# A twelve-block transformer on one core: the narrow heads' weighted values and the wide output projection, each as one TensorE step per block

## The reference

```python
h = layer_norm(x) * (1 + scale) + shift            # scale, shift from cond
q, k, v = h @ Wq, ctx_or_h @ Wk, ctx_or_h @ Wv      # split into 16 heads
a = softmax(q @ k.T / sqrt(dh))                     # 16 maps of 128 x 128
x = x + concat(a @ v) @ Wo + bo                     # gated in layer 3
...
x = x + act(h @ W1 + b1) @ W2 + b2                  # gelu, or silu(h@W1)*(h@W3)
```

## Time and profile before

| | |
|---|---|
| median of three runs | 1695.45 us |
| the profiled execution's own time | 1690.91 us |
| its span | 1688.9 us |
| TensorE matmul busy | 1518.5 us (90%), 15228 records |
| VectorE busy | 1403.1 us (83%), 3745 instructions |
| ScalarE busy | 1095.0 us (65%) |
| GpSimd busy | 911.7 us (54%) |
| mean granted TensorE clock | 0.97 of full speed |

### The profile page before, as it was taken

One profiled execution on the slowest core, in us unless ns is written; L12 is line 12 of the kernel. 1 busy time (PEld: TensorE's weight loads), 2 busy tenths in 40 slices (PEclk: granted clock), 3 DMA queues, 4 the chain that ended last, 5 costly groups with the idle time before them and its releaser, 6 DMA issues.

```text
span 1688.9 us, 40850 instructions
## 1 busy us (share of the span) xinstructions
PE 1518.5 (90%) x15228; PEld 1196.7 (71%) x15228; DVE 1403.1 (83%) x3745; ACT 1095.0 (65%) x4765; POOL 911.7 (54%) x1028
## 2 busy tenths in 40 slices
PE   6988999999889989999988989999989999989875
PEld 5876777677667777777766767776767778767653
DVE  5878788988997778898898868998898888888864
ACT  1766778657565777756576667766666686775632
POOL 3746454555765546455566646545575664554432
PEclk9999999999999999999999999999999999999975
DMA  9100000000000000000000000000000000000000
GB/s 328 37 1 2 2 2 2 7 4 4 7 8 2 2 1 2 2 7 7 6 3 7 2 2 2 2 7 1 7 7 7 2 2 2 2 2 3 3 1 3
DMA packets 14437, 20.91 MB, mean 12 GB/s; under 512 B 4064, under 2 KB 10784, under 8 KB 14240
## 3 DMA queue, kind: packets, MB, share of 16 engines
q1 hardware_dynamic: 14240, 18.31, 3.3%
HBM read 17.25 MB, written 1.05 MB: 11 GB/s over the span
## 4 chain that ended last, share of the span: by engine, by line
PE 47%; DVE 38%; POOL 8%; ACT 5%; issue 2%; DMA 0%; SPq 0%; POOLq 0%; ACTq 0%; DVEq 0%
DVE negmax L1007 9%; PE ps L665 9%; PE ps L691 6%; PE ps L552 6%; PE ps L704 5%; POOL E L859 5%; DVE E L1108 4%; ACT E L752 4%; DVE xn L967 3%; PE ps L678 3%; DVE E L1060 3%; PE ps L629 3%; PE ps L643 2%; PE ps L576 2%; PE ps L567 2%; PE ps L655 2%
## 5 line engine op out<-in xcount | busy, mean ns | idle before, releaser
L752 ACT ACTIVATE E<-ps,negmax 128x128 f32<-128x128 f32 x2048 | 719.3, 410 | 261.9 <-DVE negmax L1007 249.4
L859 POOL TENSOR_TENSOR E<-E,rinv 128x512 f32<-128x512 f32 x512 | 525.2, 1042 | 375.3 <-DVE rinv L1016 373.2
L752 ACT ACTIVATION_READ_ACCUMULATOR E<-ps,negmax 128x1 f32 x2048 | 509.7, 250 | 0.0
L1007 DVE TENSOR_REDUCE negmax<-ps 128x4 f32<-128x512 f32 x512 | 330.1, 680 | 59.3 <-PE ps L629 33.8
L665 PE MATMUL ps<-consts,E 128*128 128x128 f32 x2048 | 316.8, 285 | 39.7 <-POOL E L859 24.1
L1108 DVE COPY E<-ps 128x512 f32<-128x512 f32 x448 | 299.8, 678 | 54.6 <-PE ps L665 52.4
L665 PEld LDWEIGHTS ps<-consts,E 128*128 128x128 f32 x2048 | 233.0, 144 | 116.0 <-POOL E L859 67.6
L852 POOL TENSOR_TENSOR E<-E,prod 128x512 f32<-128x512 f32 x128 | 162.3, 1274 | 73.9 <-DVE prod L1063 72.2
L807 POOL TENSOR_TENSOR rstd<-ve,consts 128x1 f32<-128x1 f32 (+1 forms) x192 | 107.9, 563 | 83.5 <-DVE ve L960 74.0
L691 PE MATMUL ps<-E,VV 128*64 128x128 f32 x2048 | 139.4, 282 | 2.2 <-DVE E L1108 2.1
L761 ACT ACTIVATE VV<-ps 128x512 f32<-128x512 f32 x128 | 77.3, 671 | 89.8 <-PE ps L567 89.5
(11 more groups left out here) (130 smaller groups left out, 2757.1 us busy)
## 6 DMA issues: line engine op xcount, KB each, us to landing
w_f<-res_f SPq DMA_DIRECT2D x6, 256.0 KB, 11.5
qT<-in_x SPq DMA_DIRECT2D x16, 64.0 KB, 1.8
w_wq<-res_wq SPq DMA_DIRECT2D x2, 512.0 KB, 7.8
w_wk<-res_wk SPq DMA_DIRECT2D x2, 512.0 KB, 8.4
w_wv<-res_wv SPq DMA_DIRECT2D x2, 512.0 KB, 9.1
w_wo<-res_wo SPq DMA_DIRECT2D x2, 512.0 KB, 9.8
w_cq<-res_cq SPq DMA_DIRECT2D x2, 512.0 KB, 10.8
w_co<-res_co SPq DMA_DIRECT2D x2, 512.0 KB, 13.7
```

The source lines that it names most:

```text
L752: last = nc.scalar.activation(E[p][:, h, :], bank(u, j * N, (j + 1) * N), ACT.Exp, bias=negmax[p][:, h:h + 1], accum_out=sums[p][:, h:h + 1])
L859: tt(e, e, rinv[p][:, T4 * g:T4 * g + T4].unsqueeze(2).broadcast_to([N, T4, N]), ALU.mult).then_inc(done[POOL], 1)
L1007: nc.vector.tensor_reduce(negmax[p][:, T4 * g:T4 * g + T4], bank(u).rearrange("p (h m) -> p h m", h=T4), AX, ALU.max, negate=True).then_in ...
```

## The change

The four steps `MX0` to `MX3` of a narrow block become one step `MX`, which comes after all four turned groups and the values and does the same sixteen matmuls in the same order. The steps `PJ0` and `PJ1` of a wide block become one step `PJ`, which comes after both copies and does the same eight matmuls. Their costs in the plan are 1.2 (before: four of 0.45) and 1.8 (before: two of 0.9). The banks `PV` and `PJ` are now taken and completed by the same step, so the special case in `FULL` is gone. The planner makes a new order from this for all engines.

```diff
-        if k == "small":
-            add(PE, f"MX{g}", 0.45, (e, f"PT{g}"), (DVE, "V"), *([(PE, f"MX{g - 1}")] if g else []),
-                fills=() if g else ("PV",))
     if k == "small":
-        add(DVE, "PV", 0.2, (PE, "MX3"), empties="PV")
+        add(PE, "MX", 1.2, *[(turns_on(b, g), f"PT{g}") for g in range(4)], (DVE, "V"), fills=("PV",))
+        add(DVE, "PV", 0.2, (PE, "MX"), empties="PV")
...
-        add(PE, f"PJ{i}", 0.9, (ACTE, f"O{i}"), *([(PE, "PJ0")] if i else []), fills=() if i else ("PJ",))
-    add(DVE, "sum", 0.22, (PE, "PJ1"), total, empties="PJ")
+    add(PE, "PJ", 1.8, (ACTE, "O0"), (ACTE, "O1"), fills=("PJ",))
+    add(DVE, "sum", 0.22, (PE, "PJ"), total, empties="PJ")
...
-                elif step[:2] == "MX":
-                    r = int(step[2])
-                    for by, count in latest_first(EMPTY[UNIT[b, s, "V"]], EMPTY[UNIT[b, s, f"PT{r}"]]):
+                elif step == "MX":
+                    for by, count in latest_first(*[EMPTY[UNIT[b, s, n]] for n in ("V", "PT0", "PT1", "PT2", "PT3")]):
                         if fresh(pe, done[by], count):
                             pe.wait_ge(done[by], count)
-                    u = UNIT[b, s, "PV"]
                     vacated()
-                    for j in range(T4):
-                        q0 = 32 * j
-                        last = mm(ps[q0:q0 + 32, u[0], 0:N], vmask[p][:, r, q0:q0 + 32], E[p][:, T4 * r + j, :],
-                                  start=(r == 0), stop=(r == 3), tile_position=(0, q0))
+                    for r in range(T4):
+                        for j in range(T4):
+                            q0 = 32 * j
+                            last = mm(ps[q0:q0 + 32, u[0], 0:N], vmask[p][:, r, q0:q0 + 32], E[p][:, T4 * r + j, :],
+                                      start=(r == 0), stop=(r == 3), tile_position=(0, q0))
                     last.then_inc(done[PE], 1)
...
+                elif step == "PJ":
+                    for by, count in latest_first(EMPTY[UNIT[b, s, "O0"]], EMPTY[UNIT[b, s, "O1"]]):
+                        if fresh(pe, done[by], count):
+                            pe.wait_ge(done[by], count)
+                    vacated()
+                    for i in range(H // 2):
+                        _, t = tile_of(b, 2 * (i // T4), i % T4)
+                        last = mm(bank(u, 0, D), qT[p][:, i, :], W[f"{wide}o{layer}"][:, t, :],
+                                  start=(i == 0), stop=(i == H // 2 - 1))
+                    last.then_inc(done[PE], 1)
```

More of the change, by code:

```diff
@@ L282 @@
 for _b, _s, _n in UNIT:
-    _last = {"PV": "MX3", "PJ": "PJ" if KIND[_b] == "small" else "PJ1"}.get(_n)
-    _fill = next(_key for _key in ORDER[PE] if _key[2:] == (_b, _s) and (_key[1] == _last or _n in FILLS[_key] and not _last))
+    _fill = next(_key for _key in ORDER[PE] if _key[2:] == (_b, _s) and _n in FILLS[_key])
     FULL[UNIT[_b, _s, _n]] = DONE[_fill]
@@ L693, in step_of @@
                     last.then_inc(done[PE], 1)
[L694 to L706, removed]
                 elif step == "D":
@@ L715, in step_of @@
                     last.then_inc(done[PE], 1)
-                elif step == "PJ":
-                    unit = UNIT[b, s, "PV"]
-                    by, count = EMPTY[unit]
+                elif step == "PJ" and k == "small":
+                    by, count = EMPTY[UNIT[b, s, "PV"]]
                     if fresh(pe, done[by], count):
```

## The result

The changed kernel takes 1718.88 us (median of four, 1716.25 to 1720.25) against 1695.64 us for the kernel before in the same comparison: 23 us more, ratio 1.014, 95% interval 1.0118 to 1.0162. The forecast was 1676 us, with 1648 to 1712 us as its range, so the time lies outside it and on the other side of before.

What follows compares the result with a forecast made beforehand. Neither TensorE (47% of the chain of waits) nor VectorE (38%) was taken as full. From 1690.91 us, minus 25 saved, plus 6 lateness, gave 1672, plus 4.5 to the median: 1676 us; range 1648 to 1712 us.

Steps and rivals of the forecast that it cites:

- 45 us for MX: Narrow blocks' weighted values: 161 entries and exits at 0.14 + 0.14 us each leave TensorE's time, 45 us.
- 6 for PJ: Wide blocks' output projection: joining the two halves saves TensorE 0.10 us at 62 places, 6 us; ends 0 and 12.
- the exits: Time TensorE pays on leaving a lone narrow MX group, not for its matmuls: 0.14 us at each of 161 places.
- The price on entering: Transposes (L665) take 0.58 us before an MX against 0.44 before a plain step: 0.14 us more.
- the lateness: Readers behind a block's last group wait 0.64 us (narrow) or 0.9 us (wide) longer; 25 us per stream, a quarter counted.
- The share of the chain: Part of TensorE's step time on the chain of waits: 0.48 for MX, 0.6 for PJ, turning savings into 25 us of span.
- the planner isn't misled: New plan costs 1.2 and 1.8 lie near the measured 1.0 and 1.79 us, though every engine's order can change.
- The forecast's own range: Range of the main case's time, 1667 to 1690 us, from the saving's ends of 30 and 11 us.
- The slower one: Small pieces filled TensorE's gaps; put behind the last group they lengthen each stream's chain: 1710 us, chance 0.26.
- VectorE as the only bound: VectorE bounds the kernel and TensorE's time is worth nothing: 1691 to 1699 us, no change, chance 0.15.
- The bank case: PV's bank is held about 2 us instead of 6.9, so wide blocks can start earlier: 1653 us, chance 0.13.
- The signs named ahead: Forecast wrong if VectorE's waits for L678 and L704 grow over 15 us, or rounds lengthen although TensorE's busy time fell.

Runs made afterwards that it cites:

- the order of before: Steps joined at MX3's and PJ1's places, every engine otherwise ordered as in the kernel before: MX 1700.72 us, PJ 1706.44 us, both 1718.53 us.

## Why the prediction was wrong

**The saving exists, at about half its size.** The joined step was to take 1.0 us and takes 1.01. But of 45 us for MX and 6 for PJ, TensorE's busy time gave back 25 and none in the order of before, and 25.2 of 51 in the changed kernel. The 25 us are about what the exits alone come to (161 x 0.14 = 23), the low end that the prediction named. The price on entering, 0.14 us, was read from one pair of steps; over all places without idle time the transposes before an MX take 0.58 us and before another step 0.50, 0.08 us more. The Trainium skill's rule on tiling modes (TensorEngine Tiling (Array Packing), Key Properties) says that a change of the mode drains the engine, and the trace agrees again: sixteen matmuls in one mode take 1.01 us, where four lone groups took 1.44.

**The step that failed is the lateness: "So I count a quarter, 6 us. The ends are 2 us and 25 us."** With the late steps made longer by as much, it measured 30.5 us for MX and 36.1 us for PJ in the order of before, 67 us, beyond even the upper end. Two things were wrong in it. It counted the delay of the block's own stream only, and divided by four streams; but TensorE takes its steps in one fixed order, and 0.65 us more at one place hold back whatever the other three streams have queued there (in the rows at 713.13 us, another stream's weighted values). And it took the earlier trace rows as cover: VectorE waited only 5.1 us for MX. A reader's wait tells what is late now; it says nothing of how much later the step may become. With MX3 longer by 0.65 us the time rose by 30.5 us. The upper end of 25 us was also left out of the range: 11 us of saving and 25 of lateness on 1695 us are 1709 us, not 1690.

**The share of the chain was used as a price.** 0.48 for MX was too high for what left (0.23 at the early places) and too low for what came (0.73 at the late one). For the three quarters of the groups that moved, the sum should have been made by place: 64 steps longer by 0.65 us, 42 us x 0.73 = +30, and 79 us x 0.23 = -18. The joined steps kept all their matmuls, so the gain to set against the lateness is the whole early time, and not only the entries and exits. The total of both gains in the order of before was so 18 + 20 = 38 us and not 25; the lateness was eleven times too small. That its 22 us for MX (45 x 0.48) stand near the measured 18 is luck: the time freed was not 45 us and the price not 0.48.

**The order was named, and not weighed.** "Both new costs are near what the rows give (1.0 and 1.79 us), so the planner isn't misled" is no argument: a change of one cost by 0.02 moved before by 17 us. The planner's own end, at hand in both kernels, was +24.3 us for the changed one. The forecast's own range of 1667 to 1690 us had no term for it.

**The rivals.** The slower one was right in sign, at 0.26, and in mechanism as far as the order of before shows it. Its test was that the last MX of a block ends more than 0.4 us later while TensorE's share of a round falls. From the start of PT3 to the end of the last MX the mean over the 64 blocks is 3.15 us before and 3.94 after, and the share fell from 92% to 89%. Its size, 1710 us, was short: it took the same 25 us for the lateness, and 16 us for the rest without a row behind them. VectorE as the only bound is refuted by the -17.9 us of the first groups' removal and the +30.5 us of the longer MX3, both TensorE's time alone. The Trainium skill's advice beside it (Trainium Kernel Development and Optimization, Best Practices) is to judge the distance to roofline by the share of the weight loads; here that share stayed at 71% while the time rose, so it ranks no place. The bank case found no support: MX takes PV's bank only once all four groups are turned, and the rounds got longer. Its 1653 us is also 2 us off its own sum (1676 less 25).

**The signs named ahead** did their work: VectorE's waits for L678 and L704 were to grow by no more than 15 us, and grew by 5.2 + 23.0 = 28 us; rounds got longer although TensorE's busy time fell. The chain lists L674, the new line of the weighted values, no longer among its fifteen entries, so its share did fall to 2% or less, as forecast, and the kernel got slower.

## What to carry to other kernels

Where a planner writes the order, print the end of its own plan for both kernels first: here it gave the change within 2 us. Before joining steps that fill an engine's waits into one that stands at the end of a chain, price the places and not the engine: lengthen the late step by the same amount in a kernel where nothing else moves, and leave the early ones out in another. A share of the chain of waits is no price: here three quarters of a step with 3% of the chain, left out whole, gave back 17.9 us, and lengthening the rest cost 30.5. Where a greedy plan writes the order, a change of a step's cost draws a new order, and its luck (here -27 to +17 us with the steps of before) must be told from the step's effect by holding the order fixed.

## What the runs showed of the hardware

A group of four matmuls on 32-column tiles costs 0.36 us alone, and four groups in a row 1.01 us, 0.22 us for each further one. Eight full-width matmuls of the same kind take 1.79 us, 0.22 us each: a whole group for the time of one. The granted clock was lower in the changed kernel's rounds (0.97) than before (0.98 and 0.99), but the same +29 us came at 0.98 in the old order; what part of the changed kernel's time the lower clock has was not measured.
